# Two-layer graph attention on one core: a fused comparison and mask on VectorE, no zeros matmul, earlier row loads

## The reference

```python
Wh = einsum('nf,hfd->hnd', x, W)            # per head
e  = leaky_relu(s1[:, :, None] + s2[:, None, :], 0.2)
e  = where(adj > 0, e, -inf)                # mask, 4096 x 4096 for each head
att = softmax(e, axis=-1)
out = einsum('hnm,hmd->hnd', att, Wh)       # layer 0: elu, projection
x = layernorm(x + out)                      # layer 1 does the same once more
```

## Time and profile before

| | |
|---|---|
| Median of 3 runs | 3120.64 us (3114.76 to 3123.39) |
| Span of the profiled execution | 3118.6 us |
| Own time of the profiled execution | not listed apart from its span |
| Mean granted TensorE clock | 0.954 |
| Busy share PE, DVE, ACT, POOL | 89%, 72%, 68%, 21% |
| First-layer attention | about 270 to 2240 us |
| Second-layer attention | about 2478 to 3064 us |

### The profile page before, as it was taken

One profiled execution on the slowest core, in us unless ns is written; L12 is line 12 of the kernel. 1 busy time (PEld: TensorE's weight loads), 2 busy tenths in 40 slices (PEclk: granted clock), 3 DMA queues, 4 the chain that ended last, 5 costly groups with the idle time before them and its releaser, 6 DMA issues. The chain is left out here.

```text
span 3118.6 us, 76790 instructions
## 1 busy us (share of the span) xinstructions
PE 2780.7 (89%) x27212; PEld 2406.7 (77%) x27212; DVE 2232.4 (72%) x4443; ACT 2114.1 (68%) x3536; POOL 652.6 (21%) x586
## 2 busy tenths in 40 slices
PE   6885999899899899899899899899797589889892
PEld 4553888788788788788788788788686488889892
DVE  6677757756856856865865866855444599999997
ACT  3554776777678687677678687677411379889892
POOL 0003303402501600610620520500011123141400
PEclk9997999999999999999999999999898899999996
DMA  8994111101101101100100110100253311111115
GB/s 303 367 373 156 30 23 29 37 17 35 30 23 33 33 23 29 38 23 16 44 23 23 30 37 23 29 24 16 85 172 119 108 32 29 35 30 34 30 27 165
DMA packets 214904, 213.28 MB, mean 68 GB/s; under 512 B 67905, under 2 KB 177601, under 8 KB 214818
## 3 DMA queue, kind: packets, MB, share of 16 engines
q1 hardware_dynamic: 214818, 212.07, 21.9%
HBM read 161.09 MB, written 50.93 MB: 68 GB/s over the span
## 5 line engine op out<-in xcount | busy, mean ns | idle before, releaser
L674 PE MATMUL l0a_ps<-l0a_uv,l0a_b 128*128 128x258 f16 x8192 | 1848.7, 274 | 114.0 <-DVE l0a_b L783 94.2
L674 PE MATMUL l0a_ps<-l0a_uv,l0a_c 128*128 128x258 f16 x8192 | 1848.2, 275 | 0.0
L711 ACT ACTIVATE l0a_b<-l0a_s1b,l0a_kcur 128x512 fp8e4<-128x512 f32 x2048 | 1288.6, 708 | 191.4 <-PE l0a_ps L674 179.3
L674 PEld LDWEIGHTS l0a_ps<-l0a_uv,l0a_b 128*128 128x128 fp8e4 x8192 | 806.6, 98 | 242.0 <-issue 120.2
L674 PEld LDWEIGHTS l0a_ps<-l0a_uv,l0a_c 128*128 128x128 fp8e4 x8192 | 795.9, 97 | 123.9
L781 DVE SCALAR_TENSOR_TENSOR l0a_c<-l0a_b,mask_t 128x512 uint32<-128x512 uint32 x512 | 446.9, 873 | 484.2 <-ACT l0a_b L711 484.2
L674 PE MATMUL l1a_ps<-l1a_uv,l1a_b 128*128 128x130 f16 x4096 | 514.0, 223 | 45.7 <-DVE l1a_b L783 35.7
L674 PE MATMUL l1a_ps<-l1a_uv,l1a_c 128*128 128x130 f16 x4096 | 514.5, 225 | 0.0
L711 ACT ACTIVATE l1a_b<-l1a_s1b,l1a_kcur 128x512 fp8e4<-128x512 f32 x768 | 477.2, 714 | 47.1 <-DMA l1a_ncur<-l_ncol 43.3
L674 PEld LDWEIGHTS l1a_ps<-l1a_uv,l1a_b 128*128 128x128 fp8e4 x4096 | 410.5, 100 | 51.1 <-issue 50.4
L783 DVE TENSOR_TENSOR l0a_b<-l0a_b,mask_t 128x512 uint32<-128x512 uint32 x512 | 449.3, 878 | 0.0
(11 more groups left out here) (160 smaller groups left out, 2178.1 us busy)
## 6 DMA issues: line engine op xcount, KB each, us to landing
l0p_raw<-in_adj SPq DMA_DIRECT2D x128, 512.0 KB, 6.1
l_wh<-l0p_whs SPq DMA_DIRECT2D x32, 512.0 KB, 6.5
l0a_s1b<-l_srow SPq DMA_DIRECT2D x64, 256.0 KB, 3.3
l0a_whx<-l_wh SPq DMA_DIRECT2D x64, 256.0 KB, 3.5
feat<-l0a_ob SPq DMA_DIRECT2D x64, 256.0 KB, 2.4
pj_fin<-feat SPq DMA_DIRECT2D x32, 512.0 KB, 5.2
l1a_s1b<-l_srow SPq DMA_DIRECT2D x32, 256.0 KB, 2.9
l0p_xin<-in_x SPq DMA_DIRECT2D x32, 128.0 KB, 6.2
```

What stands on the lines that cost most here:

```text
L674: last = nc.tensor.matmul(sums(q, t, m), buf[k % nbuf][:, j, t * P:(t + 1) * P], row[:, 2 * m * W1:2 * (m + 1) * W1], start=first and sets ...
L711: last = act.activation(bbuf[k % nbuf][:, j, :], s1b[q][:, :], ACT.Relu, bias=kcur[q][:, jt:jt + 1], scale=STEEP, saturate=False)
```

## The change

Four edits of `attention_phase`:

- The matmul of zeros goes, with its operand. In the second layer the first real matmul of a tile on `bbuf` opens the bank (`start`) and the one on `cbuf` accumulates.
- VectorE's comparison in the second layer becomes one `scalar_tensor_tensor` that compares the float row and multiplies by the 0/1.0 mask byte. The split then covers three tiles (384 words) with its two operations, and a third one of 128 words makes the fourth tile of `cbuf` by xor of masked comparison and mask.
- SP waits for the first comparisons of block g (`s_ca`, `s_cd`) before it loads block g + 1, and stores block g - 1 after that. In both layers. The value loads of chunks 0, 1, 7 and 6 follow the store of block g - 1 and not that of block g. The blocks of the queue are written out one by one where a loop over heads stood.
- The means get a load and a semaphore of their own, and `divide` waits for it.

```diff
             def store(g):
+                h, b = g // NB, g % NB
+                sp.wait_ge(s_out, g + 2)
+                sp.dma_start(outv[:, b * TPB:(b + 1) * TPB, h * D:(h + 1) * D], ob[:, :, :]).then_inc(s_st, 16)
...
-            sp.wait_ge(s_one, 3 + sets)
+            sp.wait_ge(s_one, 4)
             load_block(0, 0, 0)
+            load_mean(0, 0)
+            load_mean(0, 1)
...
-            with sp.Fori(0, H - 1) as h:
-                head(h, False)
-            head(H - 1, True)
+            for g in range(G):
+                h, b = g // NB, g % NB
+                if g < G - 1:
+                    sp.wait_ge(s_ca, CPB * g + 1)
+                    if dve_tiles:
+                        sp.wait_ge(s_cd, CPB * g + 1)
+                    load_block((g + 1) // NB, (g + 1) % NB, (g + 1) % 2)
+                if g > 0:
+                    store(g - 1)
+                    if g < G - 1:
+                        load_mean((g + 1) // NB, (g + 1) % 2)
+                if h < H - 1 and b == 0:
+                    for m in range(4):
+                        sp.wait_ge(s_uv, h * CPB + 4 + m + 2)
+                        load_wh(h + 1, m)
...
-                            if sets == 2:
-                                nc.tensor.matmul(ps[t][q][:, 0:4 * W1], zeros[:, 0:P], zeros[:, :],
-                                                 start=True, stop=False)
...
-                                                            start=first and sets == 1,
-                                                            stop=end and m >= sets - 1)
+                                                            start=first and m < 3 - sets,
+                                                            stop=end and m >= sets - 1,
+                                                            skip_group_check=sets == 2)
...
-                        ins = dve.tensor_scalar(bbuf[k % nbuf][:, j, :], s1b[q][:, :], ncur[q][:, jt:jt + 1], None,
-                                                ALU.is_gt, saturate=False)
+                        ins = dve.scalar_tensor_tensor(bbuf[k % nbuf][:, :, :].bitcast(U8)[:, j, :], s1b[q][:, :], ncur[q][:, jt:jt + 1],
+                                                       mask_t[:, jt, bass.ds(b * BLK, BLK)],
+                                                       ALU.is_gt, ALU.mult)
...
-                if dve_tiles:
-                    dve.wait_ge(s_cd, CPB * g + (k + 1))
-                dve.wait_ge(s_ca, CPB * g + (k + 1))
-                dve.scalar_tensor_tensor(cbuf[k % nbuf][:, :, :].bitcast(U32), x, ONE8X4, m,
-                                         ALU.bitwise_xor, ALU.bitwise_and)
-                dve.tensor_tensor(x, x, m, ALU.bitwise_and).then_inc(s_bc, 1)
+                dve.wait_ge(s_ca, CPB * g + (k + 1))
+                dve.scalar_tensor_tensor(y[:, 0:ja, :], x[:, 0:ja, :], ONE8X4, m[:, 0:ja, :],
+                                         ALU.bitwise_xor, ALU.bitwise_and)
+                last = dve.tensor_tensor(x[:, 0:ja, :], x[:, 0:ja, :], m[:, 0:ja, :], ALU.bitwise_and)
+                if dve_tiles:
+                    dve.wait_ge(s_cd, CPB * g + (k + 1))
+                    last = dve.tensor_tensor(y[:, ja:JC, :], x[:, ja:JC, :], m[:, ja:JC, :], ALU.bitwise_xor)
+                last.then_inc(s_bc, 1)
```

More of the change, by code:

```diff
@@ L501, in attention_phase @@
     sets = 1 if 4 * W1 > BANK else 2
-    LOADS = 16 * (2 + (dve_tiles > 0) + elu)
+    LOADS = 16 * (2 + (dve_tiles > 0))
     assert NB % 2 == 0 and H % 2 == 0
@@ L523, in attention_phase @@
         ps = [[s.ps(f"ps{t}{m}", [P, BANK]) for m in range(2)] for t in range(TPB)]
-        if sets == 2:
-            zeros = s.sb("zeros", [P, 4 * W1], F16)
         s_pad = s.sem("pad")
         s_blk = [s.sem(f"blk{q}") for q in range(2)]
+        s_mb = [s.sem(f"mb{q}") for q in range(2)]
         s_wh = [s.sem(f"wh{k}") for k in range(4)]
@@ L564, in _ @@
             pool.sem_inc(s_uv, 1)
-            if sets == 2:
-                nc.gpsimd.memset(zeros[:, :], 0.0).then_inc(s_one, 1)
             for k in range(4):
@@ L610, in load_block, with load_mean, store @@
                         "p a t -> p (a t)")).then_inc(s_blk[q], 16)
+            def load_mean(h, q):
                 if elu:
                     sp.dma_start(mnb[q][:, :], d["mean"][0:1, bass.ds(h * D, D)].to_broadcast([P, D])
-                                 ).then_inc(s_blk[q], 16)
+                                 ).then_inc(s_mb[q], 16)
+            def store(g):
+                h, b = g // NB, g % NB
+                sp.wait_ge(s_out, g + 2)
+                sp.dma_start(outv[:, b * TPB:(b + 1) * TPB, h * D:(h + 1) * D], ob[:, :, :]).then_inc(s_st, 16)
             def load_wh(h, m):
@@ L643, in _ @@
                 load_wh(0, m)
-            with sp.Fori(0, H - 1) as h:
-                head(h, False)
-            head(H - 1, True)
+            for g in range(G):
[13 more added lines that the diff above has]
+                        load_wh(h + 1, m)
+                if h < H - 1 and b == NB - 1:
+                    for m in range(4, 8):
+                        sp.wait_ge(s_uv, (h + 1) * CPB + m - 2)
+                        load_wh(h + 1, m)
+            store(G - 1)
             sp.wait_ge(s_st, 16 * (G + 1))
@@ L681, in sweep @@
                     last.then_inc(s_pe, len(ks))
-            pe.wait_ge(s_one, 3 + sets)
+            pe.wait_ge(s_one, 4)
             with pe.Fori(0, H // 2) as hp:
@@ L747, in _, with compare @@
             dve.sem_inc(s_dv, links)
-            def compare(g, q, k, loads=None):
+            def compare(g, q, b, k, loads=None):
                 if dve_tiles:
@@ L775, in split @@
                 jt = SWEEP[q][k] * JC
+                ja = JC - dve_tiles
                 m = mask_t[:, :, :].bitcast(U32)[:, jt:jt + JC, bass.ds(b * CW, CW)]
                 x = bbuf[k % nbuf][:, :, :].bitcast(U32)
+                y = cbuf[k % nbuf][:, :, :].bitcast(U32)
+                dve.wait_ge(s_ca, CPB * g + (k + 1))
+                dve.scalar_tensor_tensor(y[:, 0:ja, :], x[:, 0:ja, :], ONE8X4, m[:, 0:ja, :],
+                                         ALU.bitwise_xor, ALU.bitwise_and)
+                last = dve.tensor_tensor(x[:, 0:ja, :], x[:, 0:ja, :], m[:, 0:ja, :], ALU.bitwise_and)
                 if dve_tiles:
                     dve.wait_ge(s_cd, CPB * g + (k + 1))
-                dve.wait_ge(s_ca, CPB * g + (k + 1))
-                dve.scalar_tensor_tensor(cbuf[k % nbuf][:, :, :].bitcast(U32), x, ONE8X4, m,
-                                         ALU.bitwise_xor, ALU.bitwise_and)
-                dve.tensor_tensor(x, x, m, ALU.bitwise_and).then_inc(s_bc, 1)
+                    last = dve.tensor_tensor(y[:, ja:JC, :], x[:, ja:JC, :], m[:, ja:JC, :], ALU.bitwise_xor)
+                last.then_inc(s_bc, 1)
             def evacuate(g, q):
@@ L797, in evacuate, with divide @@
                 fold(TPB - 1)
-            def divide(g, q):
+            def divide(g2, q):
+                g = 2 * g2 + q
                 dve.wait_ge(s_dv, (g + 1) * links + TPB)
@@ L812, in divide @@
                 ch.mark(dve.tensor_tensor(zr[:, 1, :], den, zr[:, 0, :], ALU.add))
+                dve.wait_ge(s_mb[q], 16 * (g2 + 1))
                 for t in range(TPB):
@@ L846, in body @@
                         nxt2, k2 = turns[m + 1]
-                        compare(g + nxt2, q ^ nxt2, k2, LOADS * (g2 + 1 + q))
+                        compare(g + nxt2, q ^ nxt2, bn if nxt2 else b, k2, LOADS * (g2 + 1 + q))
                     elif not last:
-                        compare(g + 1, 1 - q, ahead)
+                        compare(g + 1, 1 - q, bn, ahead)
                     if first and not nxt:
@@ L855, in body @@
                 evacuate(g, q)
-                divide(g, q)
+                divide(g2, q)
                 if elu and last:
                     add_exponentials(g + 1)
-            compare(0, 0, 0, LOADS)
+            compare(0, 0, 0, 0, LOADS)
             for k in range(ahead):
-                compare(0, 0, k + 1)
+                compare(0, 0, 0, k + 1)
                 make(k)
```

## The result

The changed kernel takes 3158.78 us (median of 4 runs, 3155.92 to 3163.87), the kernel before 3122.01 (median of 4, 3114.76 to 3124.41): ratio 1.0121 [1.0104, 1.0139], +36.8 us by the medians. The forecast was +16 us, 3137. Its direction, its place and its range hold, but its size is less than half of what was measured.

The account below looks back on a forecast made before the run. TensorE bounds the first layer; in the second, ScalarE bounds quiet blocks, VectorE those with GpSimd at work. Second-layer block groups: 3.6 + 3.3 + 5.6 + 1.5 + 1.4 + 0.6 = +16 us, giving 3137 us, range 3108 to 3168.

Parts of the forecast that it names:

- No first-layer effect: First-layer attention: expected unchanged within 3 us, with loads off the path and TensorE busy 28.0 of 28.0 us.
- the zeros matmul: TensorE, second layer: removing 14 us of work is worth 0, or 14 us if TensorE is the limit.
- Rival D: Whole kernel: no net effect, quiet turns about 1.67 us, time within 10 us of 3121; chance 0.07.
- Rival A: VectorE's second-layer turn gets no longer (1.53 us, comparison still 0.39): about 20 us saved, 3100; chance 0.13.
- B: Rival, VectorE's second-layer turn: the short fourth operation leaves gaps, costs 0.39, turn 1.93 us, total 3181; chance 0.13.
- C: Rival, first layer: GpSimd's moved chunks collide with the epilogue, TensorE stalls at seven more head changes, 3180; chance 0.07.
- The fused comparison: VectorE, second layer: costs 0.60 us (bounds 0.39 and 0.60), making the quiet turn 1.74, +0.14.
- The block's end: VectorE, second-layer block: evacuation and division 2.35 us, 0.21 more every second block, mean 2.45.
- The sum by its groups: Second-layer blocks: 7 to 14 take 147.9 us, 15 to 22 the same, 23 to 30 143.7, 1 to 6 102.4.
- In proportion to length: VectorE beside GpSimd, second layer: a 512-element operation's extra 0.43 us scales with length, slow turn 2.92 us, +0.11.
- The loads: ScalarE, second layer: 43.3 us of DMA waits vanish, leaving 16.0 us a block, but VectorE needs 16.4.
- The turn by the two prices: VectorE's quiet turn, second layer: skill's fixed-cost estimate 1.51 to 1.71 us, +0.20; trace rows, preferred, gave +0.14.

Follow-up runs that it names:

- e4: The kernel before with only the zeros matmuls removed: 3121.08 us, ratio 0.9997.
- e1: The changed kernel with the old comparison and two split operations put back, early loads and no zeros matmul kept: 3113.35 us against 3122.39 for the kernel before, 0.9974.
- e2: The kernel before with only the fused comparison and its split into three operations, loads and zeros as before: 3162.08 us, ratio 1.0130.
- e6: The changed kernel with its fused comparison against constant 0.0 instead of the per-partition threshold column: 3146.08 us, ratio 1.0086 to the kernel before.
- e5: The kernel before with each 512-word second-layer split operation cut into 384 and 128 words: 3146.28 us against 3121.03, ratio 1.0086.
- e3: The kernel before with only the new load order on SP, means on their own semaphore, value loads one block earlier: 3109.67 us, ratio 0.9967.
- e7: e1 with each second-layer split operation covering two steps (1024 words) on buffers joined in pairs: 3125.88 us, ratio 1.0017 to the kernel before.
- e9: The kernel before with GpSimd's six operations of a second-layer chunk cut into twelve of 130 elements (heads 1 to 3): 3150.38 us against 3118.57, 1.0095.

## Why the forecast had the side right and the size wrong

**Where the loss sits: right.** No first-layer effect, within the 3 us that were allowed (1.3, less than the end of that layer differs by among the kernels here); the zeros matmul worth nothing (e4); the whole loss in VectorE's turn (e1, e2). Rival D is out: there is a net effect, and without the fusion the rest gains 8 to 9 us, with it some 3 at most, which the intervals don't tell from none. Rival A is out: the turn is 0.20 longer. B is out: the short operation costs its 0.20 and leaves no gap. C is out: TensorE waits 72.5 us for VectorE in the first layer's loops, 70.7 before.

**The fused comparison: the step that failed.** The mechanism was right and this term of the sum was mis-sized most. "I take 0.60, since the fused one reads two tensors": it costs 0.66, because it also reads a column (e6). Of the forecast's two neighbours neither has two tensors and a column. 0.06 x 256 = 15 us of VectorE's work; e6 puts it at 11 us of time. The bound was wrong as well: 0.60 was called the upper end, and a pair of rows in the trace of before (0.28 and 0.35) would have shown that a column costs something.

**The block's end, the second term that was too small.** "2.45 in the mean" was carried over from before; it is 2.59, 0.14 x 31 = 4 us. Of the 0.14, 0.05 is a misreading of the kernel before (2.50, not 2.45) and 0.09 is new. The new part goes with the fused comparison. A pair of quiet blocks takes 16.77 and 17.26 us in e2, 16.29 and 16.73 in e6, so 0.44 to 0.49 apart; in e5, which has the old comparison, 16.25 and 16.56, 0.31 apart. The gap is 0.36 to 0.37 in e2 and e6, 0.21 in e1, e3, e4 and e5. TensorE, which the trace of the changed kernel names as releaser, is not the likely cause: in e2, with the same gap, the engine waits for nothing that the profile shows.

```profile
2615.74 0.75 DVE L758 SCALAR_TENSOR_TENSOR l1a_b<-l1a_s1b,l1a_ncur,mask_t 128x512 uint8<-128x512 f32 x1 [0.37 <-issue]
```

The comparison's one more address behind the loop's branch would fit, but no run tests it.

**The sum by its groups.** Blocks 7 to 14 were forecast at 147.9 and took 154.1. Of the 6.2 between them the comparison makes 8 x 8 x 0.06 = 3.8, the end 1.1 and the contention the rest, 1.3. Over 31 blocks the two quiet terms give 31 x (0.48 + 0.14) = 19 us, and 16 + 19 = 35 is near the span's 35.6. That it is so near is in part luck, for other errors cancel. Contention came out 1 us over the forecast in blocks 7 to 14 and 1 under in 23 to 30. Blocks 1 to 6 took 102.2, forecast at 102.4, but by two errors: the quiet work is 3.7 us more, and the chunks that GpSimd makes earlier have taken their 4 us of contention into block 0. The store of block 0 goes out 4.9 us later where +1.4 was said; from the first comparison to that store it is 7.5 (41.5 to 49.0), and the other 2.5 came back before the stage, whose start differs by up to 5 us among the kernels here.

**"In proportion to length": wrong rule, small harm.** The slow turn is 3.43, not 2.92, for each of its four operations is held up by 0.36 to 0.43 whatever its length (e5 and e7 show the same at other lengths). The forecast had the rows for it: in the earlier trace rows four 128-column operations lose 4.09 - 0.87 = 3.22, 0.80 each, while a 512-word one beside the same GpSimd instructions takes 1.53 in place of 0.68, 0.85. The harm is small because longer turns are also fewer in the time that GpSimd works: 41.8/3.43 = 12.2 of them, each 3.43 - 1.80 = 1.63 over a quiet one, 19.9 us a head where the forecast had 14.3 x 1.18 = 16.9. It is the same number as 48 hold-ups of 0.42. Measured: 18 by the length of the blocks and 18.3 by the count. So this step was wrong as a mechanism and right in size only because its two errors, turns too short and too many of them, nearly cancel.

The Trainium skill has a rule for this ("SBUF — State Buffer", section Who interferes with whom): a VectorE instruction with two SBUF inputs contends with a GpSimd instruction that reads SBUF, over a shared pair of ports that is an exclusive lock. Of VectorE's two-port modes it says that whoever issues first has the pair for its whole instruction and the other is blocked. The traces agree that the hold-up is one amount per instruction and follows GpSimd's length (0.21 and 0.42 us, e9), and they are the measure of its size: 0.42 where GpSimd's instruction takes 0.61 undisturbed, not all of it.

**The loads: 0 net, right here, wrong in itself.** "That takes ScalarE to 16.0 us a block without waits and no further" counted the overlap of durations and a DMA wait as work; without waits it is 15.71, and ScalarE's lead from the slow blocks makes even that no limit (e1). Nor were all of the 43.3 us of waits to be had: 12.7 remain at the start of the stage. Alone the early loads give 10 us (e3). With VectorE at 17.0 a block they give nothing measurable, as the forecast's argument has it.

**The turn by the two prices.** The estimate from the Trainium skill's fixed cost for each instruction ("VectorE: DVE Perf Modes", section on the TRN2 errata) went from 1.51 to 1.71, +0.20; measured is 1.60 to 1.80, +0.20. So the forecast set aside the difference that came true, because the level beside it was 0.09 too low. The level is 0.09 too low after the change as well, most of it, 0.06 to 0.07, at the comparison in both kernels. Both comparisons read the column, so that its price may be what drops out of the difference; for the old comparison no run tests it.

## What to carry to other kernels

On VectorE count instructions, inputs and columns before words: here fewer words per turn in one more instruction, with one wider comparison, cost 0.20 on a turn of 1.60 us. A stall taken away is worth what the next limit leaves: the same early loads gave 10 us with a turn of 1.60 and nothing that could be measured with one of 1.80. When a mean hides two regimes, look for the same operation in two lengths in each: whether a hold-up is proportional or fixed can be read from two rows, and how often it comes from a count of the other engine's instructions. And check a block's own sum by starts, not by durations and gaps: 2.35 + 0.21 stood for 2.65 here.

## What was not expected of the hardware

- A VectorE operation with two tensor inputs beside GpSimd is held up by an amount that doesn't depend on its own length (128, 384 and 1024 words: 0.42 us) but on that of GpSimd's instruction: 0.21 us at 130 elements (e9), 0.42 at 260, 0.85 at 516 (first layer, 1.53 in place of 0.68). It falls on about one VectorE operation for each of GpSimd's (46 beside 48).
- A per-partition column as an operand costs a two-tensor operation 0.06 us (0.74 and 0.68 us, 512 columns; 0.35 and 0.28, 128).
- Cutting a GpSimd operation in two is dear: 0.40 us for 130 elements, 0.61 for 260, undisturbed (e9 and the kernel before).
